# Swapping neighbouring features by two transfers instead of a matmul, and six small moves in the order of a slot

## The reference, cut to what matters

```python
q = gelu(x @ Wq.T + bq) + 0.21          # k likewise
x1, x2 = xp[..., 0], xp[..., 1]         # even and odd features
out = stack([x1 * cos - x2 * sin, x2 * cos + x1 * sin], axis=-1)
```

## Time and profile before

| | us |
|---|---|
| median of 3 runs (lowest, highest) | 1496.24 (1493.55, 1498.13) |
| the profiled execution | 1495.65 |
| its span | 1493.8 |
| TensorE busy | 1434.7 (96%) |
| TensorE weight loads | 1267.7 (85%) |
| VectorE busy | 1205.2 (81%) |
| ScalarE busy | 820.6 (55%) |
| GpSimd busy | 748.6 (50%) |

### The profile page before, as it was taken

How to read it: one execution, slowest core, us unless ns; L and a number is a source line. 1 busy time by engine, 2 the same in 40 slices (tenths; PEclk the granted TensorE clock), 3 DMA queues, 4 the chain that set the end, 5 groups by cost and what they waited for, 6 DMA issues and landing times. The chain is left out here.

```text
span 1493.8 us, 32591 instructions
## 1 busy us (share of the span) xinstructions
PE 1434.7 (96%) x10940; PEld 1267.7 (85%) x10940; DVE 1205.2 (81%) x2359; ACT 820.6 (55%) x1850; POOL 748.6 (50%) x1833
## 2 busy tenths in 40 slices
PE   8789999999999999999999999988999999898998
PEld 6658888888888888888888887867999999898998
DVE  6778889889888898898898887768888888757664
ACT  4354555454555464455555544306776777667775
POOL 1433346346355354454453451226777777467772
PEclk8889999999999999999999999998999999999999
DMA  5100000000000000000000004007777777887872
GB/s 194 61 8 8 1 15 2 14 16 1 15 15 2 16 5 12 15 5 12 16 1 15 8 1 128 2 3 174 196 193 193 191 192 195 264 315 297 312 304 75
DMA packets 135426, 130.43 MB, mean 87 GB/s; under 512 B 7232, under 2 KB 125248, under 8 KB 128768
## 3 DMA queue, kind: packets, MB, share of 16 engines
q1 hardware_dynamic: 135296, 128.79, 27.9%
HBM read 72.93 MB, written 55.84 MB: 86 GB/s over the span
## 5 line engine op out<-in xcount | busy, mean ns | idle before, releaser
L737 PE MATMUL ps_l<-ve_f,oe 128*128 128x128 f32 x2048 | 275.7, 279 | 0.8 <-DVE ve_f L1740 0.8
L737 PEld LDWEIGHTS ps_l<-ve_f,oe 128*128 128x128 f32 x2048 | 248.8, 192 | 23.1 <-issue 20.4
L1740 DVE SCALAR_TENSOR_TENSOR ve_f<-ps_s,oT 128x512 f32<-128x512 f32 x248 | 166.7, 681 | 4.1 <-PE ps_l L737 2.3
L2934 POOL TENSOR_TENSOR d_s<-d_ex 128x1024 f32<-128x1024 f32 x31 | 125.2, 4040 | 83.0 <-ACT d_ex L2684 82.8
L1701 DVE COPY_PREDICATED vals<-oh,ps_l 128x1024 f32<-128x1024 int32 x112 | 146.9, 1312 | 19.3 <-PE ps_l L477 17.4
L2559 PE MATMUL ps_s<-d_ex,arena 128*128 128x128 f32 x1024 | 121.1, 277 | 4.6 <-DVE d_ex L2827 4.6
L2559 PEld LDWEIGHTS ps_s<-d_ex,arena 128*128 128x128 f32 x1024 | 118.2, 194 | 5.0 <-DVE d_ex L2827 5.0
L2547 PE MATMUL ps_l<-arena 128*128 (+1 forms) x960 | 114.5, 279 | 3.9 <-ACT d_raw L2679 3.9
L1293 ACT ACTIVATE ve_f<-ps_l,r 128x128 f32<-128x128 f32 x128 | 47.3, 370 | 125.9 <-DVE r L1713 125.6
L2547 PEld LDWEIGHTS ps_l<-arena 128*128 128x128 f32 x960 | 111.9, 195 | 4.1 <-ACT d_raw L2679 4.1
L475 PE MATMUL ps_l<-veH,x1H 128*128 128x512 f32 x256 | 115.2, 450 | 0.1
(11 more groups left out here) (332 smaller groups left out, 3842.7 us busy)
## 6 DMA issues: line engine op xcount, KB each, us to landing
logits<-d_raw SPq DMA_DIRECT2D x128, 256.0 KB, 3.5
e_lt<-logits SPq DMA_DIRECT2D x32, 1024.0 KB, 5.1
y_slots<-d_ys SPq DMA_DIRECT2D x64, 256.0 KB, 4.6
d_ex<-y_slots SPq DMA_DIRECT2D x8, 1024.0 KB, 6.9
e_y<-y_slots SPq DMA_DIRECT2D x6, 1024.0 KB, 7.2
d_w<-W SPq DMA_DIRECT2D x16, 256.0 KB, 3.4
arena<-xT SPq DMA_DIRECT2D x16, 128.0 KB, 2.4
arena<-x SPq DMA_DIRECT2D x16, 128.0 KB, 2.4
```

The lines of the kernel that those rows point to most:

```text
L737: last = pe.matmul(ps_u[:, cols], oe[:, hp, e, :], mo[:, n % MO, hp, :], start=False, stop=(e == NE - 1 and hp == HP - 1), skip_group_chec ...
L1740: V.scalar_tensor_tensor(mo[:, n % MO, :, :].rearrange("p a n -> p (a n)"), chosen_of(b, c), float(NE - e), oT[:, u, c, :, :].rearrange("p ...
L2934: G.tensor_tensor(s8[:], part[:, 0:8, :], part[:, 8:16, :], ALU.add).then_inc(n, 1)
```

## The change

- Blocks 0 to 12 no longer have `c_rot`. SyncE gets a step `swap(b)` ahead of `store(b)`: once `c_q` of the block is done it issues two transfers that copy the odd rows of `ql` to the even rows of `t1` and the even to the odd. `c_qr` waits for both (32 increments per block of the new semaphore `c_swap`) and multiplies `t1` by sin in place. Blocks 13 to 15 keep the matmul. The minus sign goes from `rot` to the sin table.
- TensorE: `b_out(t-2, 0, 2)` moves from behind `c_out` to behind `b_out(t-2, 0, 1)`, ahead of `c_kv` and `a_op`.
- ScalarE: the copy `a_yt` goes ahead of the copy `c_kr`.
- VectorE: `b_mo(.., 0, 0)` and `b_mo(.., 0, 1)` go to the head of the slot, ahead of `b_gate`; `b_mo(.., 1, 7)` goes behind the last two convolution steps.

```diff
+            def swap(b):
+
+                sp.wait_ge(q["c_q"], b + 1)
+                wait(sp, q["c_qr"], 2 * b)
+                sp.dma_start(t1[0:P:2, :, :], ql[1:P:2, :, :]).then_inc(q["c_swap"], 16)
+                sp.dma_start(t1[1:P:2, :, :], ql[0:P:2, :, :]).then_inc(q["c_swap"], 16)
+
             def store(b):
...
+            swap(0)
             store(0)
             for pair in range(2, NB // 2 - 1):
                 for u in range(2):
                     load(2 * pair + u + 1, 1 - u)
+                    swap(2 * pair + u - 3)
                     store(2 * pair + u - 3)
             load(NB - 1, 1)
             for b in range(NB - 5, HELD):
+                swap(b)
                 store(b)
...
                 pe.matmul(linear_of(b)[:, :], rot_s[:], ql[:].rearrange("p a n -> p (a n)"),
-                          start=True, stop=True, skip_group_check=True).then_inc(q["c_rot_ps"], 1)
+                          start=True, stop=True, skip_group_check=True).then_inc(q["c_swap"], 1)
...
-                if c:
+                if c and t - 3 >= HELD:
                     c_rot(t - 3)
...
                 if o:
                     b_out(t - 2, 0, 1)
+                    b_out(t - 2, 0, 2)
                 if c:
                     c_kv(t - 3)
...
                     c_out(t - 3)
-                if o:
-                    b_out(t - 2, 0, 2)
                 if b:
                     b_turn(t - 1, 1)
...
                     b_probs(t - 1, 0)
+                if a:
+                    a_yt(t)
                 if c:
                     c_kr(t - 3)
-                if a:
-                    a_yt(t)
...
-                dve.wait_ge(q["c_rot_ps"], b + 1)
-                V.tensor_tensor(t1[:], linear_of(b)[:].rearrange("p (a n) -> p a n", a=2),
+                dve.wait_ge(q["c_swap"], 32 * HELD + b - HELD + 1 if b >= HELD else 32 * (b + 1))
+                swapped = linear_of(b)[:].rearrange("p (a n) -> p a n", a=2) if b >= HELD else t1[:]
+                V.tensor_tensor(t1[:], swapped,
                                 sin_s[:].unsqueeze(1).to_broadcast([P, 2, L]), ALU.mult).then_inc(n, 1)
...
                 t = 2 * r + u
+                if o:
+                    b_mo(t - 2, u, 0, 0)
+                    b_mo(t - 2, u, 0, 1)
                 if b:
                     b_gate(t - 1)
                 if c:
                     b_res(t - 3)
                 if a:
                     a_xd(t)
-                if o:
-                    b_mo(t - 2, u, 0, 0)
-                if a:
                     a_xst(t)
                     a_gm(t)
-                if o:
-                    b_mo(t - 2, u, 0, 1)
...
+                if more:
+                    a_conv(t + 1, 1, (3,))
                 if o:
                     b_mo(t - 2, u, 1, 7)
                 if more:
-                    a_conv(t + 1, 1, (3,))
                     a_xbc(t + 1)
...
-    rot[i[1::2], i[0::2]] = -1.0
+    rot[i[1::2], i[0::2]] = 1.0
...
+    sinT[0::2] *= -1.0
```

More of the change, by code:

```diff
@@ L331, in token_blocks @@
             b_pv b_rg b_rgs b_rgb_ps b_rgb b_ot b_m_ps b_mo b_oe b_oa b_oat_ps b_x2t_ps b_x2t b_start
-            c_qk_ps c_g c_km c_q c_v_ps c_v c_rot_ps c_qr c_t2 c_krt_ps c_kr c_kv_ps c_kv c_out_ps c_z c_res c_n
+            c_qk_ps c_g c_km c_q c_v_ps c_v c_swap c_qr c_t2 c_krt_ps c_kr c_kv_ps c_kv c_out_ps c_z c_res c_n
             c_x3t_ps c_x3t c_x3""".split()
```

## The result

The changed kernel takes 1503.66 us in the median of five runs (1502.2 to 1505.0), the kernel before in the same series 1495.96 us. The ratio is 1.0053, with a 95% interval of 1.0041 to 1.0064: slower by 0.5%. The forecast was 1504.0. The profiled execution took 1502.2 us, of which 1500.5 are the span; before it was 1493.8.

The account below looks back on a forecast made before the run. TensorE was taken to set the slot (57.29 of 57.53 us busy). Twelve slots at +0.57 (+6.8), slot 15 +0.9 and slot 16 +0.5 made +8.2 on 1495.65: 1503.85, rounded to 1504.0 us; range 1489 to 1509, its own 1500 to 1507.

Parts of the forecast that it names:

- The matmul goes, and its time turns into waiting: TensorE without c_rot: of 0.86 us removed, only 0.19 remains at c_krt, since a_yt waits for the a_cin copy.
- The transfers: The swap ahead of c_qr: both transfers land by 413.65, taken at 2.4 us, with 0.9 us to spare.
- Rival 3: The swap is late: c_qr and c_krt 1.2 us late at 4.5 us per transfer, 1518 us (1509 at 3.8); chance 0.10.
- `c_kv` and `a_op` 0.48 later: Output products and yt copy ahead of c_kv: a_op at 418.78 in place of 418.30; both engines say 418.2 for c_kv.
- Scores of heads 4 and 5 0.32 later: TensorE's b_scores start at 429.11, not 428.79; 0.41 us gained earlier is used up waiting for exponentials.
- the bound was 12.6: Sign of error: b_scores of heads 4 and 5 less than 12.6 us behind c_krt (12.54 before, 13.05 forecast).
- mo(1,7): Tile behind two convolution steps ends at 444.16; b_out(1,7) starts 0.50 us later, and stalled TensorE takes 0.05 to 0.1 to fill.
- The first two tiles: Two b_mo at the slot's head fill VectorE's wait for eg; gain taken as nothing, bounds 0 and -1.2 us a slot.
- The sum: Steady slot +0.57 us, twelve of them +6.8; slot 15 +0.9; slot 16 +0.5; in all +8.2 us.
- TensorE rules: Faster rival: TensorE keeps its 0.41 us gain at scores of heads 4 and 5, 1490.7 or 1484.5 us; chance 0.18.
- Cancel: Rival: delays meet their margins at the third tile move and a_op and cancel, 1495 to 1498 us; chance 0.14.
- Rival 4: GpSimd and c_qr's first product exclude each other, up to 0.2 us a slot, 13 times, 1506.6 us; chance 0.08.

Follow-up runs that it names:

- 1: Kernel before with the transfers in place of c_rot in the first 16 slots, all orders unchanged; slot 57.53 us, ratio 1.0014 to the kernel before.
- 5: Changed kernel with out(0,2) back behind c_out on TensorE; slot 57.97 us, ratio 1.0068 to the kernel before.
- 11: Changed kernel with the kr copy ahead of yt and mo(1,7) ahead of the convolution again; slot 57.48 us, one run, 1495.0 us.
- 7: Changed kernel with kr copy and mo(1,7) back, out(0,1) ahead of a_yt and out(0,2) behind c_krt on TensorE; slot 57.48 us, ratio 0.9999 to kernel before.
- 10: Changed kernel with mo(0,0) and mo(0,1) back behind a_xd and a_gm; slot 57.94 us in the mean, one run, 1501.4 us.
- 6: Changed kernel without the transfers, c_qr multiplying ql itself; slot 57.97 us, slot 15 52.11 us, ratio 1.0051 to the kernel before.
- 3: Changed kernel with the kr copy ahead of yt again on ScalarE; slot 57.65 us, slot 15 55.13 us, ratio 1.0051 to the kernel before.
- 4: Changed kernel with mo(1,7) ahead of the convolution (1,3) again; slot 57.80 us, ratio 1.0056 to the kernel before.
- 8: As 7, with VectorE reordered: c_res split around mo(0,6) and a maximum, later tiles and maxima earlier; slot 56.75 us, 1484.07 us, ratio 0.9934 to kernel before.
- 12: As 8, with the kr copy between the two exponentials of head 0 on ScalarE; slot 56.75 us, ratio 0.9937 to the kernel before.

## Why the prediction was right, step by step

- **The matmul goes, and its time turns into waiting.** Right, shown by 1. Forecast 0.19 us of 0.86 at `c_krt`, measured 0.29 (5.90 to 5.61); `a_yt` waits 0.56 (forecast 0.6).
- **The transfers.** 2.0 us in the median from issue to landing, taken as 2.4. An issue takes 0.47 to 0.60, where the earlier trace rows have 0.44. On time in eleven slots. The step did not allow for slots in which they land late: 0.8 us in slot 5 and 0.8 in slot 15, of the 8.3. And it read the margin of 0.9 us off a steady slot alone. In slot 15 VectorE has no convolution step ahead of `c_qr` and is free for it 3.01 us behind `c_q` (3.22 - 0.21 before, 3.79 - 0.78 after), not at 4.23; by the step's own 0.9 and 2.4 the swap lands at 3.3 and is late there, and even a pair as quick as in the steady slots (0.97 + 2.03) lands at 3.00. Rival 3 had the kind of event, in every slot in place of two.
- **`c_kv` and `a_op` 0.48 later.** Right: 0.48 and 0.47, and `a_res` 0.43. But "both say 418.2" hid which of the two it was. By 5 the `kr` copy does it alone; by 11 out(0,2) alone would have made 0.27 of it, and would still have been a gain of 0.05.
- **Scores of heads 4 and 5 0.32 later.** 0.25, and 13.08 us behind `c_krt` (forecast 13.05, the bound was 12.6). The wait of `b_turn` on the exponentials is there, 0.26 and 0.20. What TensorE had gained at the scores of heads 2 and 3 (0.51, at 11.71 in place of 12.22; forecast 0.41) is waited off; 7 shows the same mechanism with 0.94.
- **mo(1,7).** Right in kind, mis-sized: out(1,7) was forecast 0.50 later and is 0.30. VectorE reached the tile at 32.92 us of the slot, not at the forecast 33.13, because it is only 0.38 late by then and no longer 0.48. The wait for the tile is 0.05 where the sum had 0.18, and what it costs TensorE behind it 0.10, as forecast (0.05 to 0.1). So 0.32 + 0.18 + 0.07 = 0.57 became 0.25 + 0.05 + 0.10 = 0.40. That a tile without a margin passes on VectorE's pauses in three slots, 0.7 us, no term had. The first two tiles cost nothing, shown by 10.
- **The sum.** Twelve slots: forecast 6.8, measured 6.39, of which 4.8 are the twelve times 0.40, 0.8 the late swap, 0.8 the other unusual slots. Slot 15: forecast 0.9, measured 1.39, of which 0.62 are the orders (6 against before) and 0.77 the swap. Slot 16: 0.5, a value between two bounds, measured 0.48. (The 428.43 and 429.3 of the prediction for `c_kv` there stand for 928.43 and 929.3.) In all 8.2 and 8.27. So the good sum is in part luck, two errors that cancel: 2.3 us too much in the steady slots (2.0) and for the orders of slot 15 (0.3), and 2.4 us of late swaps and unusual slots that no step had. Outside this stretch the sum has nothing, and the profile has 1.43 us more ahead of slot 3 and 3.0 less behind the last `c_q`: the profiled execution took 1502.2 us, not 1503.85.
- **Rivals.** "TensorE rules" fell: 7 gives TensorE everything and the slot stays. "Cancel" fell, as neither delay met a margin. Rival 4, GpSimd and `c_qr` in each other's way, fell in its price and not in its mechanism. The first product of `c_qr` takes 0.69 us and the second starts 0.72 behind it, as before, so VectorE loses nothing; it is GpSimd that waits, and its steps had a margin (shown in the last section). Both are as the rule of the Trainium skill that spoke for it has it ("SBUF — State Buffer", "Who interferes with whom"): whichever comes second waits, and here that is GpSimd.

## What to carry to other kernels

Taking an instruction off the busiest engine buys only what the next dependency lets through. Here 0.86 us of matmul bought 0.00, 0.02 or 0.13 us, by the order around it, while a new order of the engine that held the chain (VectorE, 81% busy, not TensorE, 96%) bought 0.73 once TensorE's was in place; VectorE's alone was not tried. Before filling a wait by a reordering, look at who else stands behind the instruction that is moved: the copy of 0.59 us that went ahead of `kr` cost 0.28 us a slot, and the product for which it made room is worth 0.05. Read a margin in each kind of slot, not in the steady one alone, and count what a pause on the way does once the margin is spent. And a wait is priced from start to start, not by its bracket: 0.42 in the bracket, 0.73 in the slot.

## What the runs showed of the hardware that was not expected

**Code transfers beside a short data transfer.** DMA activity of the changed kernel over 7 us in three slots, from 530, 704 and 878 us: packets, MB, share of the engines by queue, and the median from issue to landing of the two transfers.

```profile
q1 hardware_dynamic: 160, 0.26, 9.9%
...
ve_f<-ql SPq DMA_DIRECT2D x2, 128.0 KB, 2.0
```

```profile
q1 hardware_dynamic: 160, 0.26, 10.2%
q8 instruction: 1, 0.02, 1.0%
...
ve_f<-ql SPq DMA_DIRECT2D x2, 128.0 KB, 2.6
```

```profile
q1 hardware_dynamic: 160, 0.26, 10.7%
q8 instruction: 1, 0.02, 0.8%
q14 instruction: 1, 0.01, 0.7%
```

The first is slot 9, the second slot 12, the third slot 15. Ten kernels have transfers: the changed one and 1, 3, 4, 5, 7, 8, 10, 11 and 12. `c_qr` waits for the later of the two, which is the second, so its time is given here, not the median of both:

| instruction queues with a packet beside the pair | slots | second transfer |
|---|---|---|
| none | most | 2.0 to 2.1 us |
| queue 14 | 7 and 11 | 2.3 to 2.6 us |
| queue 8 | 12, in eight kernels | 2.8 to 3.5 us |
| both | 5 and 15, in all ten kernels | 2.8 to 4.2 us |

In slot 5 the second issue is 0.4 us later as well. In runs 1 and 5 slot 12 has no such packet, and there the second transfer takes 2.03 us. `c_qr` waits in slots 5 and 15 of all ten, and in slot 12 of runs 7 and 12 alone (0.25 and 0.05 us). In the changed kernel slot 12 lands as late as slot 15, but has a convolution step of VectorE in front of `c_qr`, which slot 15 has not. The packet and the delay go together in every slot looked at; that the packet is the cause was not tried. The Trainium skill ("DMA: Bandwidth & Descriptors", "Issuing engines are not separate DMA queues") says that transfers started by ScalarE, SyncE or GpSimd run on the same 16 engines and interleave there. It doesn't speak of instruction queues in that place, and no run here shows which engines carry their packets.

**A product with two inputs in the buffer holds GpSimd up.** GpSimd's short norm steps (128x2) beside the first product of `c_qr`, in the kernel before, where the product reads PSUM and lasts from 414.78 to 415.47, and in the changed one, where it reads `t1` and lasts from 650.83 to 651.52 (the last row stands beside the second product, 651.55 to 652.24):

```profile
414.99 0.20 POOL L82 TENSOR_TENSOR rms_t<-rms_t,rms_v 128x2 f32<-128x2 f32 x1
415.27 0.19 POOL L84 TENSOR_SCALAR rms_t<-rms_t 128x2 f32<-128x2 f32 x1
```

```profile
651.05 0.52 POOL L80 TENSOR_TENSOR rms_t<-rms_y 128x2 f32<-128x2 f32 x1
651.65 0.65 POOL L82 TENSOR_TENSOR rms_t<-rms_t,rms_v 128x2 f32<-128x2 f32 x1
```

In each of the thirteen slots of the changed kernel a step that starts inside one of these products ends 0.05 us behind its end. The second product of `c_qr` always had two inputs in the buffer and holds a step to 0.70 us in the kernel before. The last of these steps, which `a_res` needs, ends 8.89 us behind `c_q` in place of 8.65, ahead of `a_res` at 9.59 (9.16 in run 8).

**A pause and the clock.** In slot 15, behind an idle stretch of 2.09 us, TensorE ran some 3.4 us at the 1.2 GHz level in one kernel (3), and behind 2.11 and 2.17 us at the full clock in two others (1 and 4).
